# Columns of Wq and Wk stored head-innermost, squares on ScalarE put back head by head

## What is computed

```python
x = _layernorm(x)                                   # the attention's input
q = _ln((x @ Wq + bq).reshape(b, s1, H, HD), qn_w, qn_b)
kv = jnp.concatenate([y_main @ Wk + bk, y_main @ Wv + bv], axis=-1)
kv = kv.reshape(b, s2, H, 2 * HD)                   # per head: 32 key columns, 32 value columns
k = _ln(kv[..., :HD], kn_w, kn_b)
v = kv[..., HD:]
ctx = _attn(qT, k.transpose(0, 2, 1, 3), v.transpose(0, 2, 1, 3)) + ctx_dca   # softmax(q k^T * SCALE) v
return ctx @ Wo + bo
```

## Time and profile before

| | |
|---|---|
| median of 3 runs | 363.45 us (363.25 to 366.77) |
| the profiled execution | 362.07 us |
| its span in the trace | 360.2 us |
| PE busy | 313.4 us, 87% |
| DVE busy | 312.0 us, 87% |
| ACT busy | 222.2 us, 62% |
| POOL busy | 173.7 us, 48% |
| granted TensorE clock | 0.979 of full speed over the span |

### The profile page before, as it was taken

One profiled execution on the slowest core, in us unless ns is written; L12 is line 12 of the kernel. 1 busy time (PEld: TensorE's weight loads), 2 busy tenths in 40 slices (PEclk: granted clock), 3 DMA queues, 4 the chain that ended last, 5 costly groups with the idle time before them and its releaser, 6 DMA issues.

```text
span 360.2 us, 7522 instructions
## 1 busy us (share of the span) xinstructions
PE 313.4 (87%) x2321; PEld 251.0 (70%) x2321; DVE 312.0 (87%) x804; ACT 222.2 (62%) x444; POOL 173.7 (48%) x261
## 2 busy tenths in 40 slices
PE   0499789799999899999999999999999999787732
PEld 0336547678888788887878787878888888586520
DVE  2977999999989899999998989998999999966564
ACT  3347987465666667676767676767585856453400
POOL 5201423337372828282828282828282827272620
PEclk9999999999999999999999999999999999989985
DMA  7980187727170909191929191819191909080002
GB/s 244 266 298 1 54 153 130 141 52 143 44 151 16 203 28 174 46 177 45 159 63 167 52 169 46 174 47 174 50 171 52 170 12 164 18 148 0 31 0 87
DMA packets 36451, 38.88 MB, mean 108 GB/s; under 512 B 8760, under 2 KB 27452, under 8 KB 36412
## 3 DMA queue, kind: packets, MB, share of 16 engines
q1 hardware_dynamic: 36044, 38.14, 49.9%
q10 hardware_dynamic: 368, 0.27, 0.3%
HBM read 16.89 MB, written 4.72 MB: 60 GB/s over the span
## 4 chain that ended last, share of the span: by engine, by line
PE 70%; issue 3%; DVE 3%; DMA 2%; ACT 1%; SPq 1%; POOL 0%; ACTq 0%; DVEq 0%
PE bank L1330 34%; PE bank L1447 13%; PE bank L1416 4%; PE bank L1594 4%; PE bank L1427 3%; PE bank L1428 3%; PE bank L1604 2%; PE bank L1501 2%; PE bank L1466 2%; DMA k_stack<-k_lo 2%; PE bank L1496 2%; PE bank L1564 1%; SPq L377 1%; DVE finals L1051 1%; ACT prob_store L750 1%
## 5 line engine op out<-in xcount | busy, mean ns | idle before, releaser
L1447 PE MATMUL bank<-v_aug,prob_store 128*128 128x66 f32 x512 | 68.2, 277 | 3.4 <-ACT prob_store L750 3.4
L517 POOL TENSOR_TENSOR k_lo<-wkv_raw,k_hi 128x448 f16<-128x448 f32 x16 | 16.8, 1047 | 107.0 <-issue 99.1
L1447 PEld LDWEIGHTS bank<-v_aug,prob_store 128*128 128x128 f32 x512 | 64.0, 194 | 5.6 <-ACT prob_store L750 4.4
L1062 DVE TENSOR_REDUCE neg_max<-bank 128x4 f32<-128x448 f32 (+1 forms) x128 | 45.2, 416 | 5.8 <-PE bank L1416 5.4
L761 ACT ACTIVATE wkv_raw<-bank,affine 128x448 f32<-128x448 f32 (+1 forms) x32 | 22.4, 749 | 39.6 <-PE bank L1496 39.3
L750 ACT ACTIVATE prob_store<-bank,exp_scale 128x512 f32<-128x512 f32 x64 | 41.6, 677 | 6.4 <-PE bank L1428 6.4
L536 POOL TENSOR_TENSOR finals<-seg_out 128x128 f32<-128x128 f32 x64 | 34.4, 546 | 13.0 <-DVE seg_out L1075 12.9
L1427 PE MATMUL bank<-q_stack,k_stack 128*128 128x128 f16 x256 | 34.7, 222 | 1.9 <-ACT maxT L612 1.9
L1428 PE MATMUL bank<-maxT,sel 128*128 128x128 bf16 x256 | 34.5, 222 | 0.0
L1427 PEld LDWEIGHTS bank<-q_stack,k_stack 128*128 128x128 f16 x256 | 26.8, 106 | 6.1 <-issue 3.9
L1075 DVE TENSOR_TENSOR seg_out<-bank,rden 128x256 f32<-128x256 f32 x64 | 27.2, 424 | 3.8 <-POOL finals L536 1.4
(11 more groups left out here) (211 smaller groups left out, 860.8 us busy)
## 6 DMA issues: line engine op xcount, KB each, us to landing
x_in<-in_x SPq DMA_DIRECT2D x16, 256.0 KB, 3.1
q_stack<-q_hi SPq DMA_DIRECT2D x32, 128.0 KB, 3.8
q_stack<-q_lo SPq DMA_DIRECT2D x32, 128.0 KB, 4.8
k_stack<-k_hi SPq DMA_DIRECT2D x32, 128.0 KB, 3.3
k_stack<-k_lo SPq DMA_DIRECT2D x32, 128.0 KB, 4.5
out<-finals SPq DMA_DIRECT2D x16, 256.0 KB, 2.7
y_dcaT<-in_x SPq DMA_DIRECT2D x8, 256.0 KB, 3.7
x_res<-in_x SPq DMA_DIRECT2D x8, 256.0 KB, 3.2
```

The costliest lines, as they stand in the source:

```text
L1062: v.tensor_reduce(neg_max[:, HG * gr:HG * (gr + 1), seg], s4[:, :, lo:hi], AX.X, ALU.max, negate=True).then_inc(max_ready.sem, 1)
L1447: last = mm(bank[6 + gr % 2][:, VW * h:VW * (h + 1)], probs[:, gr % 2, h], v_aug[:, Bt.parity, HG * gr + h], start=True, stop=True)
```

## The change

Before the launch, the host lays out three weight matrices. Wk and Wv are taken apart, so that Wk holds all key columns and Wv all value columns. The columns of Wq and Wk are stored with the head innermost, (c d g). The element counts are the same and so are the loads. In the kernel:

- `k_raw`, `q_raw`, `k_t`, `q_t` are all in the order (c d g). `head_products` reads and writes plain rows, and the scales are spread over d with the four heads innermost (`inner_wide`).
- ACT's squares (L734, L843 of before) read `k_raw` and `q_raw` in steps of four elements and write head by head, so that the sums per head are as before.
- `bias_full` is copied once with a write in steps of four elements.
- `centre_inner` replaces `centre` for Wk and Wq: its reduction reads in steps of four elements, its subtraction is on plain rows.
- the high and low parts of Wk and Wv are made from plain rows, keys wait for the load of Wk alone, values for that of Wv alone.

No instruction is added, removed or put elsewhere in any engine's order; only shapes of operands and the two waits differ. The diff, cut:

```diff
+        def by_head(ap):
+            return ap.rearrange("p (c g d) -> p c g d", g=HG, d=HD)
+
+        def head_inner(ap):
+            return ap.rearrange("p (c d g) -> p c g d", g=HG, d=HD)
...
-            for i in range(2):
-                load(wkv_in, wkv_raw[:, i], chunked((Wk, Wv)[i]))
+            load(wk_in, wkv_raw[:, 0], chunked(Wk))
+            load(wv_in, wkv_raw[:, 1], chunked(Wv))
...
-                    copy(value_half(wk_hi[:], n), key_heads(n)).then_inc(wkhi_ready.sem, 1)
+                    copy(wk_hi[:, n], wkv_raw[:, 0, n]).then_inc(wkhi_ready.sem, 1)
...
-                    s.activation(k_sq[0:MAIN], k_raw[0:MAIN, A.parity], ACT.Square).then_inc(ksq_ready.sem, 1)
+                    s.activation(by_head(k_sq[0:MAIN]), head_inner(k_raw[0:MAIN, A.parity]), ACT.Square).then_inc(ksq_ready.sem, 1)
...
-                            copy(bias_full[:, n], made[:, :]).then_inc(bias_copied.sem, 1)
+                            copy(head_inner(bias_full[:, n]), by_head(made[:, :])).then_inc(bias_copied.sem, 1)
...
-                    s.activation(q_sq, q_raw[:, A.parity], ACT.Square).then_inc(qsq_ready.sem, 1)
+                    s.activation(by_head(q_sq), head_inner(q_raw[:, A.parity]), ACT.Square).then_inc(qsq_ready.sem, 1)
...
+            def inner(ap):
+                return ap.rearrange("p (c d g) -> p c d g", g=HG, d=HD)
+
+            def inner_wide(ap):
+                return ap.rearrange("p (c g) -> p c g", g=HG).unsqueeze(2).to_broadcast([ap.shape[0], XC, HD, HG])
...
+            def centre_inner(w, means, done, parts=1):
+
+                heads = w.rearrange("p (k d g) -> p k d g", d=HD, g=HG)
+                means = means.rearrange("p (k g) -> p k g", g=HG)
+                link(v.tensor_reduce(means, heads.rearrange("p k d g -> p k g d"), AX.X, ALU.add))
+                link(v.tensor_scalar(means, means, 1.0 / HD, None, ALU.mult))
+                each = heads.shape[1] // parts
+                for part in range(parts):
+                    at = slice(each * part, each * (part + 1))
+                    v.tensor_tensor(heads[:, at], heads[:, at],
+                                    means[:, at].unsqueeze(2).to_broadcast([P, each, HD, HG]),
+                                    ALU.subtract).then_inc(done.sem, 1)
...
-                dve.wait_ge(wkv_in.sem, 16 * 2)
+                dve.wait_ge(wk_in.sem, 16)
                 for n in range(2):
-                    centre(key_heads(n), head_mean[:, 1 + n, 0:YC, 0:H // 2], wkv_centred)
+                    centre_inner(wkv_raw[:, 0, n], head_mean[:, 1 + n, 0], wkv_centred)
...
-                    v.tensor_tensor(head_inner(k_t[0:MAIN]), by_head(k_raw[0:MAIN, b.parity]),
-                                    wide(qk_small[0:MAIN, 5, 1]), ALU.mult).then_inc(kt_ready.sem, 1)
+                    v.tensor_tensor(inner(k_t[0:MAIN]), inner(k_raw[0:MAIN, b.parity]),
+                                    inner_wide(qk_small[0:MAIN, 5, 1]), ALU.mult).then_inc(kt_ready.sem, 1)
...
-                    v.tensor_tensor(head_inner(q_t), by_head(q_raw[:, b.parity]), wide(qk_small[:, 5, 0]), ALU.mult
+                    v.tensor_tensor(inner(q_t), inner(q_raw[:, b.parity]), inner_wide(qk_small[:, 5, 0]), ALU.mult
                                     ).then_inc(qt_ready.sem, 1)
```

More of the change, by code:

```diff
@@ L1627 @@
     arrays, args = {}, []
+    laid = columns_laid(inputs)
     for name in _INS:
-        a = np.ascontiguousarray(inputs[name])
+        a = np.ascontiguousarray(laid.get(name, inputs[name]))
         arrays[f"in_{name}"] = a
```

34 lines of the change are left out of this document (16 added, 18 removed).

## The result

The changed kernel takes 370.88 us (median of 6 executions, 369.66 to 374.14) beside 363.86 us for the kernel before; the ratio is 1.0198, interval 1.0153 to 1.0243. In a second comparison with more rounds it was 1.0161 (1.0110 to 1.0211). The ratios leave out executions that took over 1.5% longer than the fastest of the same kernel in the same comparison. The forecast was 365.8 us with a range of 362.9 to 368.9; the measured time lies above it. Its profiled execution took 371.13 us with a span of 369.2, where the one of the kernel before took 362.07 with 360.2.

What follows compares the result with a forecast made beforehand. PE's queue plus what is left of a DMA wait sets the pace; DVE follows. 0.43 + 0.84 - 0.37 + 0.75 + 0.42 + 0.42 = +2.5 us; on the 363.45 us median, 365.8 us, range 362.9 to 368.9.

Steps and rivals of the forecast that it cites:

- Products: DVE's thirty-two head products: 0.69 us each expected on plain rows, 13 us saved over the kernel.
- X: What reading in steps of 16 bytes adds to one ACT square: taken as 0.42 us, bounds 0 and 0.84.
- Reductions: Setup, centre_inner on DVE: stepped reads add 2.5 us, of which +0.43 sticks out past a 2.08 us wait.
- Batch 0: Start: the second square ends 0.84 us later on ACT; at most 0.37 of the products' saving arrives behind it.
- Batch 1: Start: both squares follow each other on ACT, so the sums of q start about 0.75 us later.
- first softmax step: The keys' square right ahead of the third exponential, where PE waits 1.66 us at 65.86: +0.42 us.
- The next step: The step after the first softmax step: k_raw also late, but the products' saving of about 0.4 us arrives first: 0.
- The steady part: Twelve steps from 87.00 to 308.70 us: the DMA wait swallows the delay except in one step, +0.42 us.
- (C): Rival: squares push the exponentials past the DMA wait, most steady steps losing from X = 0.67; 370.5 us at 0.84; chance 0.17.
- (B): Rival: ACT reads in steps for nothing, perhaps by a deeper read queue; 363.1 us; chance 0.17.
- (D): Rival: the head products don't get cheaper, runs of four being as bad as steps of four; 366.2 us; chance 0.05.
- (E): Rival: DVE's 87% is the bound after all and the 13 us come back; 350.4 us; chance 0.05.

Runs made afterwards that it cites:

- before_prod_plain: The kernel before with only DVE's head products written in plain rows: 363.51 us, ratio 0.9988.
- sq_write_steps: The changed kernel with the squares reading in the order of memory and writing in steps of 32 elements: 368.43 us, ratio 1.0102.
- before_a: The kernel before, unchanged, profiled once more for a further trace: 368.54 us, mean clock 0.953.
- before_b: The kernel before, unchanged, profiled once more for a further trace: 363.04 us, mean clock 0.971.
- sq_plain: The changed kernel with ACT's two squares on plain rows, all else as changed: 362.58 us, ratio 0.9983 to the kernel before.
- before_c: The kernel before, unchanged, profiled once more for a further trace: 366.57 us, mean clock 0.950.
- k_steps_only: The changed kernel with the keys' square in steps and the queries' square on plain rows: 368.88 us, ratio 1.0143 to the kernel before.
- before_sq_steps: The kernel before with only ACT's two squares reading in steps of 16 bytes: 373.34 us, ratio 1.0275.
- after: The first profiled execution of the changed kernel, with nothing further changed: 371.13 us, span 369.2.
- sq0_steps: The changed kernel with stepped squares in the first batch alone, plain rows in the other fifteen: 364.80 us, ratio 0.9994 to the kernel before.
- sq0_plain: The changed kernel with plain squares in the first batch alone, stepped in the other fifteen: 369.10 us, ratio 1.0114 to the kernel before.

## Why the prediction was wrong, point by point

*What bounds the kernel*: right as far as the runs go. DVE gets 13 us of products back and the time stays (`before_prod_plain`, 0.9988).

*Products*: right in size, 692 and 685 ns for 690 expected. What failed is the reading "DVE's busy time down by some 10 us": it went from 312.0 to 312.4. The rows of one step show where `q_lo` loses. Before, POOL's `k_lo` is nearly over when it begins (0.11 us of overlap):

```profile
205.60 1.05 POOL L517 TENSOR_TENSOR k_lo<-wkv_raw,k_hi 128x448 f16<-128x448 f32 x1 [6.75 <-issue]
206.54 0.68 DVE L1121 TENSOR_TENSOR q_lo<-wkv_raw,q_hi 128x512 f16<-128x512 f32 x1
```

After, DVE is earlier and meets it:

```profile
210.74 1.05 POOL L513 TENSOR_TENSOR k_lo<-wkv_raw,k_hi 128x448 f16<-128x448 f32 x1 [6.04 <-issue]
211.38 0.96 DVE L1130 TENSOR_TENSOR q_lo<-wkv_raw,q_hi 128x512 f16<-128x512 f32 x1
```

That is 0.41 us of overlap with `k_lo`, and `q_lo` takes 0.28 us longer. The other steps agree: in these two traces and in that of `before_prod_plain`, `q_lo` takes 0.68 us where at most 0.11 us of it lie beside `k_lo`, 0.93 to 0.96 us at 0.37 to 0.41 of overlap, and 1.11 to 1.13 us at 0.56 to 0.58. `k_lo` itself takes 1.03 to 1.06 us in the trace of before, and 1.05 in both rows above; why `q_lo` is longer beside it is not shown. `q_lo` is as long (1082 ns) in `before_prod_plain`, so it is the products that bring it, and as that run is no slower, it costs nothing that can be measured.

*Squares*: X was taken as 0.42 from DVE's write row and measured 0.515, inside the bounds of 0 and 0.84. By the prediction's own formula of nearly 6X that is 3.1 us in place of 2.5. Steps cost time in each place where a run has them, of 16 bytes except in `sq_write_steps`, whose writes go in steps of 32 elements: ACT's read (621 to 1135 ns), ACT's write (1104 ns in `sq_write_steps`), DVE's read (680 to 1038) and DVE's write (685 to 1101), 0.36 to 0.52 us for 512 elements.

*Reductions*: 1038 and 3829 ns for 1100 and 4000. The +0.43 can't be seen: with them in and the squares plain, DVE's first `k_raw` starts at 27.00 us, in the middle of before's 25.89 to 28.08, and batch 1's mark stands at 66.22. The wait of 2.08 us that was to cover the rest was no fixed thing: in `before_a` and `before_b` DVE doesn't wait there at all.

*Batch 0*: its +0.84 is right in kind and came as 1.0. From DVE's first `k_raw` to its sum of the queries' squares it is 5.12 us in all four traces of before and in `sq_plain`, and 6.12 and 6.13 in the two of the changed kernel: 2X, with X = 0.5. DVE's wait at 33.20 grew by more, from 1.38 to 2.90, because DVE had come to it earlier:

```profile
33.11 0.69 DVE L1103 TENSOR_REDUCE qk_ss<-wkv_raw 128x16 f32<-128x512 f32 x1 [2.90 <-ACT wkv_raw L839]
...
54.43 0.66 PE L1475 MATMUL bank<-ident,x_norm 128*128 128x128 f32 x4 [2.01 <-ACT sel L608]
67.61 2.30 PE L1456 MATMUL bank<-v_aug,prob_store 128*128 128x66 f32 x16 [1.15 <-DVE seg_out L1084]
```

PE's wait for the selectors, 0.76 us in the first trace, is 2.01 here; in `before_a` and `before_c` it is 1.55 and 1.67. The third of these rows is the weighing behind the third exponential. The profile names `seg_out` as what it waited for, but by the code this weighing needs only the first `seg_out`, which is over at 66.40. The third exponential starts at 66.89; with the 0.67 us that one takes elsewhere it ends at an estimated 67.56, just ahead of the weighing at 67.61, as in the kernel before (65.14 + 0.67 = 65.81 and 65.86).

*Batch 1 and the first softmax step* lie ahead of batch 1's mark. From DVE's `k_raw` in the first softmax step to that weighing it is 1.98 us before (63.88 to 65.86) and 2.47 after (65.14 to 67.61): the forecast's +0.42, at 0.49. With batch 0 these terms were 0.84 - 0.37 + 0.75 + 0.42 = 1.64 us, or 2.1 with X = 0.515; the full-clock traces add up to 1.6.

*The next step* (from batch 1's mark to batch 2's) was put at 0, because the products' saving of about 0.4 us would bring `k_raw` earlier. It doesn't: `k_raw` comes 14.36 us behind batch 1's mark before, 14.46 with cheap products alone and 14.44 in `k_steps_only`. The square then adds its 0.50 us to PE's wait.

*The steady part* (+0.42): 0.6 us over the mean of before's four traces, and the eight traces with stepped squares of the keys and cheap products average 220.0 us against 219.3 for those four, 0.7. The DMA wait swallows the rest, as the prediction said: by its formula PE's delay is X - 0.27 = 0.25 us a step, 2.9 us in twelve, and 5.0 us of waiting became 1.9 (1.1 in the second trace). The step to batch 15 was not in the sum; with filler it is 0.15 us longer than in the first trace (18.01 and 17.86). And the square of the queries, priced at nothing in the steady part, cost at most a little, ratio 1.0033.

*The step that failed.* The mechanism held, the square of the keys ahead of the third exponential and both squares on the path of the start. At full clock its parts are an estimated 1.6 us up to batch 1's mark, 0.5 in the next step, 0.7 in the twelve and 0.15 behind them, together 3.0 us, where the sum had 2.5. That these are so near each other is partly luck: the 0.43 of the reductions didn't show, and the 0.50 of the next step, put at nothing, did. But the kernel loses 5.5 us (12 executions against 84) to 7.0 (the medians of the result), and the other 2.5 to 4 us are in no term. What failed is that the prediction held PE's busy time fixed ("PE's busy time the same") and priced every delay at its own length. PE's busy time went from 313.4 to 323.5 us, with the same work (318.6, 315.4 and 318.7 in the three further traces of before): at 54 and 66 us PE already stands for 0.76 and 1.66 us, and for 1.56 at 315, and behind such stands the matmuls can run at half the clock (0.50 from 70 to 74 us and from 322 to 335 us in the first trace of the changed kernel). The step to batch 2 takes 22.1 us in the changed kernel's traces against 19.9 at full clock, and that to batch 15 19.6 against 18.0. The kernel before pays this as well, but less: over its four traces the mean is 20.1 and 18.8 us.

A smaller part is the ground the sum was put on. 363.45 us was the median of three executions; the mean over the later comparisons is 364.4 us for the 67 executions that enter the ratios and 365.1 for all 84, 0.9 to 1.7 us higher. So of the 5.1 us between the forecast and 370.88, 0.9 to 1.7 are the ground, about 0.5 the squares' own delays, and the remaining 2.9 to 3.7 what comes on top of them, of which the clock is the part that the traces show.

*The rivals.* (C), the exponentials past the DMA wait, was priced from X = 0.60 on; at 0.515 it hasn't begun in the changed kernel. But it is real: where the products stay dear, `before_sq_steps`, PE waits 12 times for that exponential and twelve steps take 4.6 us more. In the steady part the two kernels differ in little but the products, which points to their saving as what keeps the change from it, a link that the prediction didn't have there. (B), (D) and (E) are out: squares of 1140 ns, products of 690, and 0.9988 for the products alone. The deeper read queue that (B) thought possible for ACT was a guess of mine, and no run shows one.

*What stays open.* How much of the part on top is clock. By marks, the two traces of the changed kernel lose an estimated 2.5 us to it beyond what before's four lose (0.3 in the start, 1.5 in the step to batch 2, 0.7 in that to batch 15), and with the 3.0 at full clock that is 5.5 of their 5.9 us. But both have a mean clock of 0.945, which only one other of its 12 executions has; the rest have 0.949 to 0.969. By mean clocks over all executions it is 0.6 to 1.0 us, and then some 2 us of the 4.9 to 5.2 at equal clock are explained by nothing here. The parts by batch (0.9994 and 1.0114) and by square (1.0143 and 1.0033) don't decide it, their intervals being 0.4 to 0.6% to either side. Nor is it shown what in one execution starts the fall of the clock in the start; a wait of 1.65 to 1.69 us at 66 us stood ahead of both outcomes.

## What to carry to other kernels

A layout that saves one engine's stepped access mostly hands the steps to another; price it where it arrives, on the engine that feeds the bottleneck, and not by the busy time it frees: here 13 us off an engine that waits anyway were worth nothing that could be measured, and half a microsecond ahead of an exponential, once a batch, cost 1.4%. Look at the granted clock of several executions before taking one trace as the ground of a sum, and where the bottleneck already stands for a microsecond or two, expect that an added delay may cost more than its length (a step of 22.1 us where it takes 19.9 at full clock). Where such a stand can't be removed, filling it with matmuls is a cheap probe of what the clock takes there; too many of them delay the start by themselves (71.41 against 69.71 us).

## What the runs showed of the hardware

- ACT pays 0.48 to 0.52 us for 512 FP32 elements read in steps of 16 bytes or written in steps of 32 elements (631 to 1147 ns and 621 to 1104 ns); a copy out of PSUM that comes to write in steps of 16 bytes goes from 584 to 1112 ns. For steps of 16 bytes DVE pays less, 0.36 to 0.40 us on a read (680 to 1038 ns, 676 to 1071 ns) and 0.40 to 0.42 on a write (1088 and 1101 against 692 and 685 ns).
- A stand of PE of 2.14 us was followed by a clock of 0.50 for some 13 us (`after`, 322 to 335 us), and a filled one of the same place by none; but in `sq0_steps` and `sq0_plain` an unfilled one of 2.15 us was followed by the full clock as well (1.00 for 6 us and more). At 66 us stands of 1.65 to 1.69 us were followed by a fall in three traces (`before_a`, `before_c`, `sq0_steps`) and one of 1.66 us by none; nor was one of 2.18 us in `before_sq_steps` (68.15 us, clock 1.00 from 66 to 80). The length of a stand alone doesn't tell whether the clock falls.
- Whether one longer wait is worse than two short ones, the runs don't show. In the tail, the traces of before have PE wait 0.42 us for DVE's maxima and then 1.56 for ACT's copy, and take 17.86, 18.54, 19.34 and 19.58 us to batch 15; where the products are cheap the first wait is gone and the second is 2.14 or 2.15 us, and the eleven such traces take 17.72 to 19.66.
